# Attention block with routed experts: the gated products stay in the PSUM bank

## The reference, cut to what matters

```python
x = layernorm(x + attention(x))          # x: 4 x 1024 tokens of 256 channels; 16 query heads on 8 key/value heads
x = layernorm(x + ffn(x))
# ffn: 64 experts, top 6 per token, capacity 768 rows each, hidden width F = 176,
#      and one shared expert of width 352 for every token
scores = softmax(x @ gate_w.T); topk_w, topk_idx = top_k(scores, 6)   # weights normalised to sum 1
g = einsum('ecd,efd->ecf', buf, w_gate)
u = einsum('ecd,efd->ecf', buf, w_up)
eo = einsum('ecf,edf->ecd', silu(g) * u, w_down)                      # the change touches silu(g) * u
y[token] += eo * weight                                               # scatter-add over the 6 experts of a token
return y + shared_swiglu(x)
```

## Time and profile before

| | |
|---|---|
| median of 3 runs | 2543.48 us |
| the profiled execution | 2551.08 us, its span 2549.3 us |
| busy share of the span | PE 90%, POOL 62%, DVE 54%, ACT 48% |
| chain that ended last | PE 53%, POOL 16%, issue 12%, DVE 9%, ACT 5%, DMA 4% |
| L2039, indirect adds of rows on POOL | 458.4 us busy, 264 instructions |

### The profile page before, as it was taken

How to read it: one execution, slowest core, us unless ns; L and a number is a source line. 1 busy time by engine, 2 the same in 40 slices (tenths; PEclk the granted TensorE clock), 3 DMA queues, 4 the chain that set the end, 5 groups by cost and what they waited for, 6 DMA issues and landing times.

```text
span 2549.3 us, 34748 instructions
## 1 busy us (share of the span) xinstructions
PE 2296.0 (90%) x11880; PEld 1786.2 (70%) x11880; DVE 1383.8 (54%) x2884; ACT 1227.5 (48%) x2323; POOL 1585.3 (62%) x1422
## 2 busy tenths in 40 slices
PE   5999999999999899999999999987798999989961
PEld 3777776777767677776667767665677888778751
DVE  2444444455574454557445455735567776656644
ACT  3444444444444344443434444333335777667744
POOL 2566555544578654447864445784443888888885
PEclk8999999999999899999999999999998999999986
DMA  3766721121113112111311211222437988878756
GB/s 123 301 243 259 276 74 63 48 70 59 45 61 117 59 53 74 53 40 65 123 50 52 89 39 39 71 83 90 165 125 219 215 205 195 191 175 200 165 78 219
DMA packets 152695, 310.35 MB, mean 122 GB/s; under 512 B 26528, under 2 KB 88224, under 8 KB 152512
## 3 DMA queue, kind: packets, MB, share of 16 engines
q1 hardware_dynamic: 104176, 252.05, 29.6%
q0 software_dynamic: 48192, 55.68, 11.7%
q10 hardware_dynamic: 144, 0.33, 0.0%
HBM read 168.01 MB, written 149.34 MB: 124 GB/s over the span
## 4 chain that ended last, share of the span: by engine, by line
PE 53%; POOL 16%; issue 12%; DVE 9%; ACT 5%; DMA 4%; POOLq 0%; another core or an unknown queue 0%; SPq 0%; ACTq 0%; DVEq 0%
PE bank L769 33%; PE bank L1117 12%; POOL y_part L2039 8%; POOL nacc L1990 4%; PE bank L1127 3%; POOL slots L2029 3%; DMA y_part<-y_e,row_token 2%; PE bank L779 2%; PE bank L1114 1%; DVE acc L1653 1%; ACT a L1370 1%; DVE ub L1618 1%; DVE yt_lo L1632 1%; ACT yt_hi L1381 1%; ACT a L1374 0%
## 5 line engine op out<-in xcount | busy, mean ns | idle before, releaser
L1990 POOL TENSOR_TENSOR nacc<-nacc,a 128x512 f32<-128x512 f32 (+1 forms) x384 | 447.9, 1166 | 292.4 <-ACT a L1374 140.1
L1117 PE MATMUL bank<-a,v 128*128 128x512 f32 x1024 | 529.5, 599 | 3.9 <-DVE nrm L1638 3.6
L2039 POOL DMA_INDIRECT y_part<-y_e,row_token x264 | 458.4, 1736 | 119.8 <-issue 77.5
L1370 ACT ACTIVATE a<-bank,c_s 128x512 f32<-128x512 f32 x384 | 263.3, 686 | 171.5 <-PE bank L769 133.8
L769 PE MATMUL bank<-q_hi,k_hi 128*128 128x512 f32 (+1 forms) x640 | 324.5, 507 | 12.5 <-ACT a L1370 6.2
L1374 ACT ACTIVATE a<-ub 128x512 f32<-128x512 f32 (+1 forms) x256 | 133.9, 523 | 393.8 <-DVE ub L1618 375.6
L1990 POOL TENSOR_TENSOR nacc<-a,a 128x512 f32<-128x512 f32 (+1 forms) x128 | 148.9, 1163 | 259.8 <-ACT a L1370 199.1
L2029 POOL DMA_INDIRECT slots<-rows,slot_u x192 | 197.6, 1029 | 138.3 <-DVE slot_u L1780 86.7
L1653 DVE SCALAR_TENSOR_TENSOR acc<-bank,rec,acc 128x256 f32<-128x256 f32 x512 | 223.5, 478 | 95.6 <-PE bank L769 87.9
L769 PE MATMUL bank<-q_lo,k_hi 128*128 128x512 f32 (+1 forms) x640 | 239.8, 375 | 0.0
L769 PE MATMUL bank<-q_hi,k_lo 128*128 128x512 f32 (+1 forms) x640 | 238.2, 372 | 0.0
(11 more groups left out here) (215 smaller groups left out, 5656.7 us busy)
## 6 DMA issues: line engine op xcount, KB each, us to landing
slots<-acc SPq DMA_DIRECT2D x65, 816.0 KB, 7.6
w_raw_f<-in_wffn SPq DMA_DIRECT2D x66, 624.0 KB
xr<-slots SPq DMA_DIRECT2D x64, 544.0 KB
decay_all<-decay_dram SPq DMA_DIRECT2D x128, 128.0 KB
w_hi<-w_dram SPq DMA_DIRECT2D x24, 384.0 KB
w_lo<-w_dram SPq DMA_DIRECT2D x24, 384.0 KB
sum<-y_part SPq DMA_DIRECT2D x16, 512.0 KB, 10.0
wc_hi<-wc_dram SPq DMA_DIRECT2D x24, 256.0 KB
```

What stands on the lines that cost most here:

```text
L1117: e.matmul(dst, v[n % 3][:, s, :], a32[u % NA][:, :, :], start=first, stop=False, skip_group_check=True).then_inc(s_av)
L1370: e.activation(squares, score_bank(u)[:, 0:R * w].rearrange("p (r t) -> p r t", r=R), ACT.Square, scale=c_s[b % 2][:, g * (g - 1) + s, h:h ...
L1990: e.tensor_tensor(out_, a, b, op).then_inc(s_nadd)
L2039: e.indirect_dma_start(out=y_part[part], out_offset=bass.IndirectOffsetOnAxis(ap=token, axis=0), in_=y_e[y][:, j, :], in_offset=None, boun ...
```

## The change

`h_a` and `h_b` are no longer SBUF tiles but names for parts of the PSUM banks. DVE writes silu times up over the up part (for `h_b`: over the gate's last 48 rows, partitions 0 to 47 of the third bank). ACT's rounding and DVE's subtraction read the bank. TensorE may then start job `k` only when both subtractions of job `k - 2` are done (`c_hl`), in place of the waits for `c_silu` and `c_h`; DVE's two waits for its own earlier subtractions go. No instruction is added, removed or moved on any engine.

```diff
-            h_a = sb(ffn, "h_a", [P, MAIN])
-            h_b = sb(ffn, "h_b", [FB, MAIN])
 def gate_up(k, part):                                   # TensorE
-                once.wait_ge(c_silu, 2 * (k - 1))
-                once.wait_ge(c_h, 2 * (k - 1))
+                once.wait_ge(c_hl, 2 * (k - 1))
 def hidden_part(k, part, width):                        # ACT
-                    e.activation(ha_hi[i][:, 0:width], h_a[:, 0:width], ACT.Copy).then_inc(c_hh)
+                    e.activation(ha_hi[i][:, 0:width], bank[b0 + 1][:, 0:width], ACT.Copy).then_inc(c_hh)
-                    e.activation(hb[i][0:FB, 0:width], h_b[:, 0:width], ACT.Copy).then_inc(c_hh)
+                    e.activation(hb[i][0:FB, 0:width], bank[b0 + 2][0:FB, 0:width], ACT.Copy).then_inc(c_hh)
 def hidden_part(k, part, width):                        # DVE
+                h_a, h_b = bank[b0 + 1][:, 0:width], bank[b0 + 2][0:FB, 0:width]
-                    once.wait_ge(c_hl, 2 * k - 1)
-                    e.tensor_tensor(h_a[:, 0:width], bank[b0 + 1][:, 0:width], silu_a[:, 0:width], ALU.mult).then_inc(c_h)
+                    e.tensor_tensor(h_a, h_a, silu_a[:, 0:width], ALU.mult).then_inc(c_h)
-                    once.wait_ge(c_hl, 2 * k)
-                    e.tensor_tensor(h_b[:, 0:width], bank[b0 + 2][FBO:KB, 0:width], silu_b[:, 0:width], ALU.mult).then_inc(c_h)
+                    e.tensor_tensor(h_b, bank[b0 + 2][FBO:KB, 0:width], silu_b[:, 0:width], ALU.mult).then_inc(c_h)
-                    e.tensor_tensor(ha_lo[i][:, 0:width], h_a[:, 0:width], f32(ha_hi[i][:, 0:width]), ALU.subtract).then_inc(c_hl)
+                    e.tensor_tensor(ha_lo[i][:, 0:width], h_a, f32(ha_hi[i][:, 0:width]), ALU.subtract).then_inc(c_hl)
-                    e.tensor_tensor(hb[i][FBO:KB, 0:width], h_b[:, 0:width], f32(hb[i][0:FB, 0:width]), ALU.subtract).then_inc(c_hl)
+                    e.tensor_tensor(hb[i][FBO:KB, 0:width], h_b, f32(hb[i][0:FB, 0:width]), ALU.subtract).then_inc(c_hl)
```

More of the change, by code:

```diff
@@ L1250, in over_body @@
                 e.wait_ge(c_wl, raw_loads + q - KJ + 1)
-                e.wait_ge(c_silu, 2 * (k - 1))
-                e.wait_ge(c_h, 2 * (k - 1))
+                e.wait_ge(c_hl, 2 * (k - 1))
                 for part in range(3):
```

## The result

The changed kernel takes 2501.08 us (median of 4 runs, 2498.7 to 2508.49), the kernel before 2543.09 us (4 runs, 2539.32 to 2544.66) on the same chip. The ratio is 0.9842, 95% interval 0.9818 to 0.9865: 42.0 us less. Forecast were 2500 us and 43.6 us less.

The account below looks back on a forecast made before the run. POOL's queue of adds was taken to bound the expert stage. Held time -44, new wait +1.5 and ACT's bank reads -1.1 gave -43.6 us, from a median of 2543.5 to 2500 us; range 2490 to 2532.

Parts of the forecast that it names:

- The bound: Expert stage: POOL's queue of adds, four a job, sets the end; 50.5 us of the adds' 458.4 are extra.
- No real wait: POOL's adds from about 1955 us to the last: only 0.30 us of issue behind each, no real wait.
- (a): Expert stage: `ha_lo` and `hb` with one SBUF input stop holding adds; 44 us less on POOL, 6 us held time left.
- The walk: Add starts counted from `wf_lo`'s end: 1.73, 3.58, 5.43, 7.28 us after the change, so four adds fit each job.
- The lower bound of the gain: Whole kernel: only the 30.1 us of `h_b`/`ha_lo` and `hb` gone, with 2.6 lost, giving 2516 us.
- (b): Expert stage afterwards: POOL and PE equal per job, `y_e` no longer slows PE, overflow weights still late, tail unchanged.
- (c): DVE in expert jobs: at most 20 ns more per instruction, 6.7 us in all, and later `ha_lo` starts, all hidden.
- (d): ACT reading a bank: 632 to 598 ns, hidden in the expert stage, 1.1 us less in the shared stage.
- (e): TensorE's new wait: nothing added in the expert stage, 1.5 us in the shared stage, bounds 0 and 2.6.
- The holding stays: Rival, expert stage: differing input and output partitions hold adds, still seven in two jobs; no gain, 2543 us; chance 0.09.
- another limit: Rival: DMA capped at 0.89, or the wait and DVE's later starts counting in full; 2520 us; chance 0.12.
- a longer hold: Rival, expert stage: adds starting in `h_b` held to the end of `hb`, 18 us more, 2562 us; chance 0.06.

Follow-up runs that it names:

- experiment 4: Changed kernel plus a 0.69 us DVE instruction with two SBUF inputs behind `ha_lo` in each expert job; 2502.57 us, ratio 0.9847.
- experiment 5: Changed kernel plus a 0.69 us DVE instruction with one SBUF and one bank input behind `ha_lo` in each expert job; 2504.35 us, ratio 0.9851.
- experiment 1: Changed kernel with `h_b` alone back in SBUF; 2528.95 us against 2556.2 for the kernel before, ratio 0.9899.
- experiment 2: Changed kernel with `h_a` alone back in SBUF; 2519.24 us against 2556.2 for the kernel before, ratio 0.986.
- experiment 6: Changed kernel plus a 0.69 us DVE instruction with two SBUF inputs behind `hb` in each expert job; 2502.89 us, ratio 0.9849.
- experiment 3: Kernel before with only TensorE's new wait (`c_hl` in place of `c_silu` and `c_h`); 2553.45 us against 2556.2, ratio 0.999.
- experiment 12: Changed kernel with POOL's eight fetches of overflow rows moved from jobs 32 to 35 to job 2; 2527.03 us against 2555.01, ratio 0.9902.
- experiment 9: Changed kernel plus two DVE instructions with two SBUF inputs per expert job, one ahead of `ha_lo`, one behind it; 2537.23 us, ratio 0.9931.
- experiment 7: Changed kernel itself, run again on a further chip; 2535.21 us against 2555.29 for the kernel before, ratio 0.9919.
- experiment 10: Changed kernel plus two DVE instructions with one SBUF input per expert job, one ahead of `ha_lo`, one behind it; 2537.49 us, ratio 0.9927.

## Why the prediction was right, point by point

**The bound.** Right. POOL's adds set the end of the expert stage though POOL is 62% busy over the span; there are 41.5 us less of them, and the time fell by 42.0. That these two agree so closely is partly luck, since the shared stage and the tail moved as well. "No real wait" from 1955 us on was nearly so: POOL had three longer gaps, of 1.57, 2.76 and 0.41 us. The rule that an add is held to an end 1.42 us after the end of the DVE instruction in which it starts (for `h_b`, of the `ha_lo` behind it) holds in all kernels run. The Trainium skill ("SBUF — State Buffer", Who interferes with whom) ties it to a second SBUF input of the DVE instruction; experiments 4 and 5 agree, 25 held against none of 53.

**(a), the held time.** Forecast 44 us off POOL, measured 41.5 in the adds' own time and 43.3 in their stretch. What is left was set at 6 us and is 9.0 (416.9 - 264 x 1.545). The walk gave the starts as they are: 1.85 us apart, the fourth in the last 0.1 to 0.2 us of `wf_lo`. One thing in the working was not right: it booked 30.1 us to `h_b` and `hb` as if each removed its own part. Experiments 1 and 2 show that either subtraction alone brings nearly everything (525.8 and 527.8 us against 524.3), because what was lost was the step, seven adds in two jobs where eight fit. The lower bound of the gain in the prediction, all but `wf_lo`'s 19.2, was therefore too careful.

**(b), what is next late.** Right: ACT's wait for `y_e` fell from 52.8 to 10.7 us (windows of 380 and 330 us), the overflow weights still come late (18.8 us the longest, before 22.0), DMA is at the 0.94 that was worked out, and held nobody. The tail did not keep its length: 44.3 us, before 41.5.

**(c), DVE's durations.** `ha_lo` 678 to 691 ns, `h_b` 701, `ha_lo` starting 0.73 after `h_b` in place of 0.61: as forecast, and off the path. Experiments 4 to 6 put a whole 0.69 us a job on DVE for nothing.

**(d)** ACT's rounding fell from 632 to 599 ns, as forecast. Its 1.1 us on the path can't be told apart.

**(e), the new wait.** Forecast 1.5 us, bounds 0 and 2.6. The place is right, the price not to be seen. The third shared job's first product (before 1798.76, behind `h_b`) now stands behind `hb`:

```profile
1800.72 0.77 PE L767 MATMUL bank<-xe_hi,wf_hi 128*128 128x512 f32 x1 [7.95 <-DVE hb L1799]
```

It is 1.96 us later, but in the changed kernel's profile the stage as a whole ends earlier, and experiment 3 has 0.999 (0.9977 to 1.0003) with the wait alone. The end of the last add, forecast at 2464, is 2455.96: those 8 us are the ones ahead of the first add. No term of the prediction gave them.

**The rivals.** "The holding stays" is refuted by the changed kernel and experiment 1, "another limit" by POOL's bare 0.30 us of issue behind each add at DMA 0.94, "a longer hold" by 48 free adds in `hb`.

**What the prediction did not see.** It had the shared stage within 3 us of before. That it went 10 us down on one chip and about 18 up on others is outside its terms, and so are the freed scatters. The changed kernel was run again on one of the slower chips: 2535.21 against 2555.29 us, 20.1 us less where 43.6 were forecast, ratio 0.9919; experiment 12 on another has 0.9902. The term for the adds came out on both (stretches of 524.9 and 516.3 us). That the whole time came out too is luck of the first chip, on which the shared stage did not take the gain back.

## What to carry to other kernels

Look for the engine that never waits in the stage, whatever its mean share, and compare its slowest instances of one kind with what the other engines do at their starts; a fixed distance to another engine's end gives the cause away. Where two loops have nearly the same period (here 7.40 and 7.41 us), ask what restores the step rather than summing the holds: here one freed instruction of two was nearly enough. Profile a change on more than one chip before its ratio is believed, since another stage may move the other way.

## What the runs showed of the hardware that was not expected

- Only the instruction in which an add starts counts. Adds that start in `h_a` are free although `wf_lo` follows (26 before, 50 after, none held), and an add that starts in the last 0.13 us or so of `wf_lo` is free too. One that starts in the 0.09 us in which `wf_lo` has begun and `h_a` has not ended is held, and takes 2.8 us (three of them in experiment 2). The 0.13 us and the 1.42 us are one fact, as far as these rows go: 1.545 - 1.42 = 0.125, and for the scatter, which ends 0.86 us behind the end of what holds it, 0.985 - 0.86 = 0.125. So an estimate from these rows is that the held part of either begins some 0.13 us behind its start.
- There is one exception: an add that starts in `h_b` is held to the end of a two-SBUF `ha_lo` behind it (22 of 23 before, one of two in experiment 2). Those not held start within 0.04 us of the start of `h_b`; the held ones start 0.07 us behind it or later. Four scatters that start in `h_b` are held in the same way. The same does not happen from `h_a` into `wf_lo`, nor from `ha_lo` into an added two-SBUF instruction (experiment 9). `h_b` reads the bank from partition 64 and writes partition 0. A shift between partitions is not enough: in experiment 6 `hb` reads partitions from 0 and writes from 64, with a two-SBUF instruction behind it, and of the 53 adds that start in it none is held. What it is about `h_b` was not tried.
- On two chips (experiments 7, 9, 10 and 12) PE's down products of 128x256 had 18 to 22 gaps between them, 15 to 19 us in all, the products up to 1.40 us apart or more, with POOL's scatter issued every 1.29 us beside them, where the first chip ran them 0.12 us apart.
